# Attention and experts of a gated block: the work on batches 1 to 7 moves from in front of body 0 into the first nine bodies

## The reference

```python
xn = _layernorm(x, axis=-1)
s = _L0_attn_ref(xn, W_qkv, W_out)                  # 32 query heads, 16 k/v heads of 64, ALiBi, causal
g = _silu(_L0_ffn_ref(xn, gate_w, gate_b, w1, b1, w2, b2))
x = x + s * g
# in _L0_ffn_ref, 8 experts, 2 per token:
gate_logits = x @ gate_w + gate_b
topk_vals, topk_idx = jax.lax.top_k(gate_logits, K)
topk_w = jax.nn.softmax(topk_vals, axis=-1)
h = jax.nn.gelu(x @ w1[e] + b1[e], approximate=False)
y = h @ w2[e] + b2[e]                               # summed over the token's two experts with topk_w
```

## Time and profile before

| | us |
|---|---|
| median of three runs | 1181.03 (1179.85 to 1181.83) |
| the profiled execution | 1181.91 |
| its span, first to last instruction | 1180.2 |

### The profile page before, as it was taken

One profiled execution on the slowest core, in us unless ns is written; L12 is line 12 of the kernel. 1 busy time (PEld: TensorE's weight loads), 2 busy tenths in 40 slices (PEclk: granted clock), 3 DMA queues, 4 the chain that ended last, 5 costly groups with the idle time before them and its releaser, 6 DMA issues.

```text
span 1180.2 us, 48395 instructions
## 1 busy us (share of the span) xinstructions
PE 1099.3 (93%) x16933; PEld 874.3 (74%) x16933; DVE 934.1 (79%) x3095; ACT 945.0 (80%) x1926; POOL 863.8 (73%) x972
## 2 busy tenths in 40 slices
PE   2679989999999999998999879999999999999996
PEld 1457767777777777777888757878878888778875
DVE  8768878888788888886777758888888888888884
ACT  3567878888888888886666558888888888888884
POOL 7067878888888888886000038999999999989995
PEclk9989999999999999999999989999999999999998
DMA  8635876666667666664435425656676676666654
GB/s 241 224 78 120 141 147 132 141 138 131 133 125 140 137 135 136 135 131 90 95 83 101 101 68 119 134 133 136 138 135 136 137 139 137 136 133 136 136 136 67
DMA packets 278630, 153.16 MB, mean 130 GB/s; under 512 B 185424, under 2 KB 266880, under 8 KB 277760
## 3 DMA queue, kind: packets, MB, share of 16 engines
q1 hardware_dynamic: 274032, 141.54, 57.6%
q0 software_dynamic: 4096, 8.40, 2.7%
q10 hardware_dynamic: 272, 0.13, 0.0%
HBM read 15.76 MB, written 16.91 MB: 28 GB/s over the span
## 4 chain that ended last, share of the span: by engine, by line
PE 78%; DVE 5%; SPq 5%; POOL 3%; issue 3%; ACT 3%; DMA 2%; ACTq 0%; DVEq 0%; POOLq 0%
PE ps L1023 10%; PE ps L997 9%; PE ps L941 8%; PE ps L943 7%; PE ps L942 7%; PE outs L1055 6%; PE ps L1027 6%; PE outs L1059 6%; PE outs L1057 6%; PE ps L1024 4%; PE ps L1032 3%; POOL t_lo L866 3%; PE outs L942 1%; PE outs L941 1%; PE outs L943 1%
## 5 line engine op out<-in xcount | busy, mean ns | idle before, releaser
L866 POOL TENSOR_TENSOR t_lo<-stage 128x512 f16<-128x512 f32 x640 | 653.0, 1039 | 133.8 <-ACT stage L1331 127.5
L1331 ACT ACTIVATE stage<-ps,slope 128x512 f32<-128x512 f32 (+1 forms) x768 | 451.2, 616 | 69.2 <-PE ps L1032 64.2
L1626 DVE CUSTOM_DVE_ANT_0 stage<-ps,kmask 128x512 bf16<-128x512 f32 (+7 forms) x1024 | 417.4, 452 | 29.7 <-PE ps L997 18.7
L1023 PE MATMUL ps<-q_st,k_st 128*128 128x256 f16 (+3 forms) x1024 | 299.0, 299 | 6.6 <-ACT stage L1331 3.4
L1055 PE MATMUL outs<-v_sp,stage 128*128 128x65 f16 x2560 | 273.0, 194 | 15.7 <-DVE stage L1656 9.7
L1057 PE MATMUL outs<-v_sp,stage 128*128 128x64 f16 x2560 | 273.1, 193 | 0.0
L1059 PE MATMUL outs<-v_sp,t_lo 128*128 128x65 f16 x2560 | 272.9, 193 | 0.0
L1055 PEld LDWEIGHTS outs<-v_sp,stage 128*128 128x128 bf16 x2560 | 236.2, 98 | 32.7 <-issue 12.7
L1057 PEld LDWEIGHTS outs<-v_sp,stage 128*128 128x128 bf16 x2560 | 235.0, 98 | 7.4
L1059 PEld LDWEIGHTS outs<-v_sp,t_lo 128*128 128x128 f16 x2560 | 235.4, 98 | 0.0
L1024 PE MATMUL ps<-q_st,k_st 128*128 128x128 f16 x1024 | 223.3, 218 | 0.0
(11 more groups left out here) (222 smaller groups left out, 2688.9 us busy)
## 6 DMA issues: line engine op xcount, KB each, us to landing
q_st<-stage SPq DMA_DIRECT2D x256, 128.0 KB
k_st<-stage SPq DMA_DIRECT2D x128, 128.0 KB, 2.4
q_st<-stage SPq DMA_DIRECT2D x256, 64.0 KB
k_st<-stage SPq DMA_DIRECT2D x128, 64.0 KB, 1.9
slot_y<-stage SPq DMA_DIRECT2D x39, 128.0 KB, 2.2
slot_x<-att SPq DMA_DIRECT2D x2, 2048.0 KB, 9.1
X<-in_L_attn_inputs SPq DMA_DIRECT2D x4, 512.0 KB, 9.7
stage<-in_L_attn_W_qkv SPq DMA_DIRECT2D x2, 1024.0 KB, 7.1
```

Source lines behind the costliest of these rows:

```text
L866: pool.tensor_tensor(t_lo[r], t_p[r], upper(t_p[r]), ALU.subtract).then_inc(s[f"lo{u % NG}"], 1)
L1023: pe.matmul(d, k[:, 0, at], q[:, 0, seen], start=(c0 == 0), stop=False, skip_group_check=True)
L1331: e = act.activation(t_p[r][:, c0:c1], S_ps[u % 2][:, c0:c1], ACT.Exp, scale=slope[:, bass.ds(pair_index(n) * 2 * SLOTS + sl * 2 + h, 1)])
L1626: ins = dve.tensor_tensor_reduce(junk[b][:, c0:c0 + w], M_ps[b][:, c0:c0 + w], kmask[:, SEQ - w:SEQ], -1.0 / 1024, 3e38, ALU.add, ALU.min, ...
```

## The change

- **Inputs.** x comes in four unequal loads (4, 8, 8, 12 tiles; the third issued by ScalarE), w_qkv in six: what bodies 0 and 1 need first (`FIRST_W`), the rest later (`REST_W`); all into `att`, which is no longer cleared. The first body of each batch writes `att` instead of adding.
- **Normalising and turning.** Batch 0 as before on VectorE and TensorE. Of batches 1 to 7 GpSimd normalises three tiles in four and ScalarE one, in place; ScalarE and GpSimd split the rows (`rows_hi`, `rows_lo`), and a DMA transpose on SP (`turn_batch`) makes `xT` of them; TensorE transposes none.
- **Order.** D tasks of body 0 come right behind its q_hi. The waits of the first rough round for all batches and of the first P for `kept` are gone. Gate products stand in TensorE's window 1 (`gates`), ranks in window 4; choose in bodies up to 4, route in 6 to 9 (two pieces of route in later bodies, as before). w_out is split behind E3 and E5 of body 1.
- **Constants.** COPIES and the zeros (from a small blank tile, five DMAs) are issued by ScalarE.
- **Sends.** Bodies 9 to 30, in slots D0, D1 and the new D2, one each, three in 20 of the 22 bodies.
- **weights_lo.** On VectorE, as one operation that scales and subtracts; ScalarE's second activation goes.
- **FILL.** The rounds of body 32 are spread over parts 8 to 25 instead of 20 to 28, the peaks and D tasks accordingly, and C0, K0, K1 on SP are two to four parts earlier.

The core of the diff:

```diff
         "DVE": [
-            ("A0", 0, 81), ("Q0", 2, 87), ("O0", -2, 98), ("N1", 0, 98),
+            ("A0", 0, 81), ("W0", 0, 82), ("Q0", 2, 87), ("O0", -2, 98), ("N1", 0, 98),
         "POOL": [
-            ("L8", -1, 6), ("L9", -1, 7), ("L0", 0, 10), ("L1", 0, 10), ("D1", 0, 38), ("L2", 0, 48), ("D0", 1, 59),
-            ("L3", 0, 64), ("L4", 0, 72), ("W0", 0, 75), ("L5", 0, 78), ("L6", 0, 81), ("L7", 0, 89),
+            ("L8", -1, 6), ("L9", -1, 7), ("D2", 0, 10), ("L0", 0, 10), ("L1", 0, 10), ("D1", 0, 38),
+            ("L2", 0, 48), ("D0", 1, 59), ("L3", 0, 64), ("L4", 0, 72), ("L5", 0, 78), ("L6", 0, 81),
+            ("L7", 0, 89),],
-AHEAD = {"PE": ("K0", "Q0", "Q1", "V0"), "ACT": ("K0", "Q0", "Q1", "V0"), "DVE": ("K0", "Q0", "Q1", "V0"),
+AHEAD = {"PE": ("K0", "Q0", "Q1", "V0"), "ACT": ("K0", "Q0", "Q1", "V0", "D0", "D1"), "DVE": ("K0", "Q0", "Q1", "V0"),
     "PE": {
-        ("M0", -1): 20, ("M1", -1): 21, ("M2", -1): 22, ("K0", -1): 22, ("M3", -1): 23, ("M4", -1): 24,
-        ("M5", -1): 24, ("C0", -1): 25, ("M6", -1): 25, ("Q0", -1): 26, ("M7", -1): 27, ("M8", -1): 28,
-        ("Q1", -1): 28,
+        ("M0", -1): 8, ("M1", -1): 9, ("M2", -1): 12, ("K0", -1): 12, ("M3", -1): 13, ("M4", -1): 16,
+        ("M5", -1): 17, ("C0", -1): 20, ("M6", -1): 20, ("Q0", -1): 23, ("M7", -1): 24, ("M8", -1): 25,
+        ("Q1", -1): 25,
     "DVE": {
-        ("B0", -1): 20, ("B1", -1): 23, ("B2", -1): 23, ("B3", -1): 23, ("B4", -1): 25, ("B5", -1): 26,
-        ("K0", -1): 26, ("B6", -1): 26, ("Q0", -1): 29, ("B7", -1): 29, ("B8", -1): 29, ("Q1", -1): 29,
+        ("B0", -1): 10, ("B1", -1): 11, ("B2", -1): 14, ("B3", -1): 15, ("B4", -1): 18, ("B5", -1): 19,
+        ("K0", -1): 19, ("B6", -1): 22, ("Q0", -1): 27, ("B7", -1): 28, ("B8", -1): 28, ("Q1", -1): 29,
...
+        FIRST_ONES = {"SP": [("C1", 0), ("Q0", 1), ("C0", 1), ("K0", 2), ("Q1", 1), ("A0", 0)],
+                      "DVE": [("B0", 0), ("B5", 1),
+                              ("B4", 3), ("B8", 3), ("B2", 4), ("B5", 4), ("B8", 4),
+                              ("V0", 6), ("V0", 7), ("K0", 8), ("V0", 8), ("B0", 9), ("B1", 9),
                               ("N1", HALF - 2), ("A1", HALF - 2), ("A1", HALF - 1)],
+                      "PE": [],
+                      "ACT": [("C0", 0), ("Q0", 1), ("D0", 1), ("C1", 0), ("E0", 0), ("E1", 0), ("E2", 0),
+                              ("E4", 0), ("E6", 0), ("E8", 0), ("W0", 1), ("E1", 1), ("E3", 1), ("E5", 1), ("E7", 4),
+                              ("C0", HALF + 1)],
+                      "POOL": [("L0", 0), ("L1", 0), ("L2", 0), ("L3", 0), ("L4", 0),
+                               ("L4", 1), ("L5", 1), ("L6", 1), ("L7", 1)]}
...
+        def rest_hi(i):
+
+            name, src, hi, _ = REST_W[i]
+            nc.scalar.wait_ge(s[name], 16)
+            nc.scalar.activation(hi, src, ACT.Copy, scale=WS)
+            nc.scalar.activation(src, src, ACT.Copy, scale=WS).then_inc(s["rest_hi"], 1)
+
+        def rest_lo(i):
+
+            _, src, hi, lo = REST_W[i]
+            nc.gpsimd.wait_ge(s["rest_hi"], i + 1)
+            nc.gpsimd.tensor_tensor(lo, src, hi, ALU.subtract).then_inc(s["rest_lo"], 1)
...
+            TURNS = ((1, 2), (3, 4), (5,), (6,), (7,), (0,))
...
+                    sp.wait_ge(s["rowlo"], q)
+                    sp.dma_start_transpose(xT[:, q * QT:(q + 1) * QT, :, :].rearrange("p t a c -> p (t a) c"),
+                                           x_rows[:, q * QT:(q + 1) * QT, :].rearrange("p t c -> p (t c)"))\
+                      .then_inc(s[f"back{q}"], 16)
...
+            expert_constants()
+            rest_lo(K_REST)
+            rest_lo(V_REST)
+            for q in range(1, NB):
+                normalise_rows(q)
+            rest_lo(Q_NEXT)
+            for q in range(1, 4):
+                rows_lo(q)
+
+            def early(k):
+
+                if k < 4:
+                    rows_lo(k + 4)
+                elif k == 4:
+                    rest_lo(Q_REST)
+                else:
+                    in_between(k - 5)
...
+            def gates():
+
+                bank_free(GATED, "O0")
+                pe.wait_ge(s["gate_w"], 1)
+                for t in range(NT):
+                    if t % QT == 0 and t > 0:
+                        pe.wait_ge(s[f"back{t // QT}"], 16)
                     gate_product(t)
...
+            act.dma_start(X[:, 3 * QT:5 * QT, :], x.rearrange("b (t p) d -> p (b t) d", p=P)[:, 3 * QT:5 * QT, :])\
+               .then_inc(s["x2"], 16)
+            for i in (K_PART, Q_PART, V_PART):
+                split_hi(i)
             roots(0, 0, QT)
-            split_hi(K_PART)
-            split_hi(V_PART)
-            turned_hi(0)
-            split_hi(Q_PART)
+            turned_hi()
+            act.wait_ge(s["rows"], ROW_STEPS)
+            for to, made in COPIES:
+                act.dma_start(to, made).then_inc(s["copied"], 16)
             bodies_of_half[:] = 0, HALF
...
             for sl in range(SLOTS):
                 q_hi(0, 0, sl)
+                spread_heads(0, 0, sl)
             v_hi_part(0, 0, 0)
             roots(1, QT, NT)
             act.preload_act_table(ACT.Exp)
...
+            rest_hi(K_REST)
+            rest_hi(V_REST)
             act.wait_ge(s["b1tr"], 1)
             act.copy(b1T[:, :], ps[4][:, 0:E * FC]).then_inc(s["b1"], 1)
...
+                if k == 0:
+                    rest_hi(Q_NEXT)
+                    rows_hi(1)
+                    rows_hi(2)
+                elif k < 6:
+                    rows_hi(k + 2)
+                elif k == 6:
+                    rest_hi(Q_REST)
+                elif k < 12:
+                    if k == 7:
+                        act.wait_ge(s["blank"], 1)
+                    zero_rows(k - 7)
+                elif k == 12:
+                    act.wait_ge(s["wo"], 16)
+                    act.activation(wo_hi[:, :, :].rearrange("p j d -> p (j d)"), wo_in, ACT.Copy, scale=WS)
+                elif k == 13:
+                    act.activation(wo_in, wo_in, ACT.Copy, scale=WS).then_inc(s["wo_hi"], 1)
+                else:
+                    keep_ranks()
...
+            def weights_lo(n, _par, _):
+
+                dve.wait_ge(s["w_hi"], n + 1)
+                dve.scalar_tensor_tensor(out=wx_chunk(wx_lo, n), in0=raw_chunk(n), scalar=WS, in1=wx_chunk(wx_hi, n),
+                                         op0=ALU.mult, op1=ALU.subtract).then_inc(s["w_lo"], 1)
```

More of the change, by code:

```diff
@@ L841, in send @@
             def send(n, _par, k):
[L844 to L847 removed]
+                for t, k in sent_with(n, k):
                     if (t, k) == (0, 0):
                         pool.wait_ge(s["routed"], 1)
[L850 to L851 removed]
+                        pool.wait_ge(s["zeros"], ZEROS)
+                        pool.wait_ge(s["back0"], 16)
                     pool.nop(nofuse=True)
@@ L888, in add_expert @@
                 pool.tensor_tensor(m, m, y_now[1][par][:, :], ALU.add).then_inc(s["added"], 1)
-            sends = {"L": lo_part, "D": send, "W": weights_lo}
+            sends = {"L": lo_part, "D": send}
             enter_bodies("POOL", sends, 0, HALF)
-            run_bodies("POOL", {**sends, "Y": in_between}, 0, HALF)
+            run_bodies("POOL", {**sends, "Y": early}, 0, HALF)
             leave_bodies("POOL", sends, 0, HALF)
```

436 lines of the change are left out of this document (222 added, 214 removed).

## The result

The changed kernel takes 1189.9 us (median of 4 runs, 1186.7 to 1191.4) against 1180.6 before (4 runs): 1.0076 times as long, interval 1.0059 to 1.0094. It is slower by 9, where 30 less were forecast. The profiled execution took 1189.27, with a span of 1187.5 against 1180.2.

What follows compares the result with a forecast made beforehand. TensorE was not the bound before body 0's sum; VectorE's choose and route pieces delayed it, then TensorE's 14.85 us per body. 17.3 + 4 + 3.9 + 5.1 = 30.3 off 1181.9 gave 1151.6 profiled, median 1151; range 1143 to 1160.

Steps and rivals of the forecast that it cites:

- A: Start to the first split of exponentials on GpSimd: comes 17.3 us earlier, at 45.5 instead of 62.81.
- the nearest is 0.29 for the same number of columns on 8 partitions: 6.1: Ahead of the first split: GpSimd normalises 21 tiles in 6.1 us, costed from an 8-partition row of 0.29.
- B: First split of exponentials to body 0's sum: 4 us shorter, a loss of 10.1 instead of 14.1.
- beside the bodies' own 109 GB/s: First split to first sum: zeros, gates and w_out adding up there was the long bound, 3 us longer.
- rival 2: Bodies 0 to 2: zeros and COPIES in ScalarE's DMA queue delay the stacks, +10 us, 1161; chance 0.1.
- The 9.5 of stalls: First split to first sum: 9.5 us of waits and half clock go, 4.6 still lost.
- The 5.5: First split to first sum: ScalarE's excess work in windows 0 and 1, 6.5 us less 1, lengthens the path.
- C: First sum to body 25: 3.9 us shorter, 9.9 of stalls gone against ranks and choose/route pieces added.
- nine pieces of choose/route ahead of peaks, 0.3 each: 2.7: First sum to body 25: choose/route pieces placed ahead of peaks add 2.7 us in all.
- rival 1: Start comes early, but moved work is paid back between slots TensorE waits on: 14 us, 1169; chance 0.2.
- D: Entrance of the second half: new FILL makes it 5.1 us shorter by removing waits and a clock drop.
- Rival 3: First half: weights_lo on VectorE sits on the chain, 1.5 us in 32 bodies, 49 us, 1200; chance 0.03.

Runs made afterwards that it cites:

- norm_on_vector: Changed kernel with the 21 tiles GpSimd normalised done by VectorE instead, behind its scales of the later tiles; 1.0049 of the kernel before.
- pool_tiles_imm: Changed kernel with constants 0 and 1 as operands of GpSimd's 21 tiles, leaving them unnormalised; 1.0130 of the kernel before, total time not comparable.
- norm_gate: Changed kernel with the 21 tiles on VectorE and the gate's weight scaling and comparison mask ahead of the bodies; 1.0032 of the kernel before.
- three_fixes: norm_gate with the five clearing transfers issued by ScalarE behind its table load instead of between body 0's exponentials; 1.0023 of the kernel before.
- zeros_early: Changed kernel with the five clearing transfers issued by ScalarE behind its table load instead of between body 0's exponentials; 1.0178 of the kernel before.
- gate_early: Changed kernel with VectorE's scaling of the gate's weights and the comparison mask moved ahead of the bodies; 1.0062 of the kernel before.
- pool_clear: three_fixes with the five clearing transfers issued by GpSimd instead of ScalarE; 0.9945 of the kernel before.
- pool_clear_root: pool_clear with ScalarE's square root of the first batch ahead of the three weight splits instead of behind them; 0.9913 of the kernel before.
- before_fill_w0: Kernel before with the new FILL table and the experts' weights' remainder on VectorE, ScalarE's second copy dropped; 0.9956 of the kernel before.
- before_fill: Kernel before with only the new FILL table, the changed order of the second half's entrance; 0.9949 of the kernel before.

## Why the prediction was wrong, point by point

**A (17.3 forecast, 7.1 measured).** The rebuilt queues were right up to GpSimd's tiles: first maximum at 28.41 (28.3 forecast), GpSimd free at 34.95 (34.9), even the second table load. The term that failed is "the nearest is 0.29 for the same number of columns on 8 partitions: 6.1". The 21 tiles took 16.36; the 10.2 us missed are this one term. The forecast's upper bound of 0.45 did not reach it either: it had no row of the form and took the most favourable neighbour, although VectorE's own rows and GpSimd's 1.16 for 512 columns with two inputs could have warned it. norm_on_vector and pool_tiles_imm show the cause. The seven issues of COPIES lasted 1.83 + 2.63 us, where 6.2 was allowed.

**B (-4 forecast, +17.7 measured).** Of the causes below the forecast had one, the clearing, and had it too cheap.
- The clearing: "beside the bodies' own 109 GB/s" was weighed as ScalarE's issue time of 0.65 each and not as a full set of DMA engines in front of the stacks. Moving it away shortened the stretch by 9.0 (norm_gate against three_fixes) and by 5.3 (the changed kernel against zeros_early). This is rival 2's mechanism, which named the zeros; it was given 10 us and a chance of 0.1, and set aside because stacks are issued a body ahead.
- VectorE's starved instruction: not among the terms. gate_early shortened the stretch by 4.2 (69.7 to 65.5). The rule was quoted, and used only for W0, 0.4 us at a time.
- What is left in pool_clear is 59.1, still 7.1 above before. TensorE's idle time in it is as long as before's (59.13 - 49.11 = 10.0; 52.04 - 41.58 = 10.5); its busy time is 7.5 longer. 3.4 of these are the gate's products (from 80.00 to 83.35 in pool_clear_root; 3.8 in the forecast). For the rest, ten more matmuls and a clock of 0.89 against 0.93 lie in the stretch; this was not taken apart further. The 9.5 of stalls that were to go did not shorten the idle time: other waits took their place. The forecast had also read 7.8 us of waits on peaks as part of this stretch; they were counted from 43.9, and only one, of 2.0, lies behind 62.81. The 5.5 that it did add, for ScalarE, no run shows: TensorE's six longest waits from 55.7 to 125.4 in the changed kernel name VectorE, a DMA, GpSimd or no one.
- The granted clock was 0.67 and 0.59 from 20 to 40 and from 40 to 60, where it was 1.00 before. TensorE was busy 10.7 to 11.7 of 20 us in both windows of both kernels, so its busy time does not tell why, and the cause is not shown. Ahead of the first split it matters little, as far as norm_on_vector and norm_gate show: 0.61 and 1.00 from 20 to 40, with the first split at 49.5 and 50.6. Behind the split it may matter more: 0.80 was granted over the stretch of the changed kernel and 0.93 before, and TensorE was busy 51.3 us against 41.6, of which the gate's products are 3.4; no run separates the clock's part.

**C (-3.9 forecast, +5.6 measured).** The half on the sends was right: no body of 16.0 is left, and bodies 7 to 25 take 2.1 less, with a pitch of 14.92 instead of 14.85 that before_fill_w0 pins on the weights' remainder, "costed at nothing". The failed term is "nine pieces of choose/route ahead of peaks, 0.3 each: 2.7". A piece is mostly two to four instructions, of 0.2 to 1.1 each. From O 3 to O 4 (177 to 196) VectorE has two pieces of route; the dearest rows of these:

```profile
L1668 DVE TENSOR_TENSOR wx_lo<-wx_lo,per_e 128x256 f32<-128x256 f32 x1 | 1.1, 1082 | 0.0
L1666 DVE TENSOR_SCALAR per_e<-per_e 128x8 f32<-128x8 f32 x1 | 1.0, 1011 | 0.0
L1665 DVE TENSOR_TENSOR per_e<-per_e 128x8 f32<-128x8 f32 x1 | 0.7, 652 | 0.0
```

With their neighbours the two are 4.2 us, not 0.6, and that interval is 18.77 long, 3.9 over the floor, with VectorE busy 17.2 of it and TensorE 15.3. The interval of the ranks (143 to 162) is TensorE's: 18.89 busy of 19.08, 4.2 over the floor where 3.3 were allowed. O 0 to O 7 takes 118.0 to 120.1 in every variant of the changed kernel, whatever was done ahead of it, and 118.0 in all seven with the shorter bodies. So this loss goes with the moved work itself, paid inside bodies in which VectorE had 2.5 of 14.86 us free. That is rival 1. It is read from the rows: no run moved or removed a piece.

**D (-5.1 forecast, -7.1 measured).** Right in mechanism, and before_fill shows it alone (-6.9). The clock was 1.00 from 675 to 690; waits of 1.4 and 1.1 us stayed (667 to 712), where none over 1 was forecast.

**Rival 3** was rightly put low as it stood. **The sum.** The forecast was wrong by 39 us, or 37.7 by the profiled executions: by these runs 10.2 for the tiles, 9 for the clearing, 4.2 for the starved instruction, 8.5 for the rest of B and 9.5 for C, less 2 that D and 1.7 that the other stretches gave beyond the forecast. The losses overlap (norm_gate; the clearing alone gave 5.3), so this is a division and not a sum of independent causes; the first three have runs of their own, C is read from rows, and the 8.5 is open.

## What to carry to other kernels

Work taken out of a serial start and put into a pipeline whose engines are 80 to 90% busy was here paid again in full (O 25 at 497.6 in pool_clear, 495.2 in before_fill). Each piece should have a gap that the trace shows; count a piece by its instructions, each with its own row. Before an engine is given work in front of a chain, find a row of that very form, operand kinds and partitions, and if there is none, take the bound from the dearest neighbour. A transfer that nobody waits for still has a place and an issuer: here the same five transfers cost 5 to 9 us among the stacks, 11 of blocked ScalarE when issued early there, and 1.3 at the first split from an idle engine while the others wait for inputs.

## What the runs showed of the hardware that was not expected

- A GpSimd TENSOR_SCALAR on a 128x128 float32 tile takes 0.78 us with two operands read for each partition and 0.61 with constants; an 8x128 one takes 0.29. VectorE takes 0.39 for the first form. The Trainium skill (GPSIMD Engine Reference, engine selection) calls one-input work there roughly line-rate; by these rows GpSimd takes twice VectorE's time for the first form.
- A VectorE instruction with all its data in SBUF can be kept off by a gapless run of GpSimd instructions to the end of the run: 8.59 us for 128x8, 3.87 for 128x256. It need not be: in norm_on_vector four such instructions, 0.67 to 2.06 each, got in between the members of a run.
- Issues of 1.28 MB transfers from ScalarE: 0.40 for the first, about 2.5 each for the next, during which ScalarE does nothing else; 0.36 to 0.40 each in the changed kernel, where exponentials stand between them; from GpSimd 0.94 each.
- Bodies with three sends have two stable lengths, 14.92 and 15.3 us, seven kernels each, and most of these have the same instructions from body 7 on. Two sends gave 14.92 where three gave 15.36. Each length is read from one profiled execution. What chooses between them stays open, and with it about 8 us of any change in front of body 7; a comparison that leaves out the length of a steady body can mislead by that much.
